# Preparing the weights of nine stages one stage earlier, in a chain of transformer layers on one core

## The reference

```python
h = tokens(x)                                    # sin/cos features times a matrix, class token in front
h = h + mixer_and_mlp(layernorm(h))              # layer 1
h = h + attention_and_experts(layernorm(h))      # layer 2
h = h + spiking_attention(layernorm(h))          # layer 3
h = h + attention_and_mlp(layernorm(h))          # layer 4

# layer 1:  x += mixer(rms(x) * g) @ w_out;  x += gelu(rms(x) * g @ ff_w1 + b1) @ ff_w2 + b2
# layer 2:  x += softmax(q k / 4) v @ out_proj.T + b, 12 heads of 16;  then 8 experts, the best 2 of each token
# layer 3:  branch(u, i) = spike(bn(u @ W[i].T + b[i]) / 2 - 1), bn of stored mean and variance
#           q, k, v = branches 0 to 2;  xa = (q k') v;  out = branch(spike(xa), 3)
# layer 4:  as layer 2's attention; the second half of the batch is a sum of three variants of fewer channels,
#           weighted by gumbel_weights[i]; then an MLP, for the second half again three weighted variants
```

## Time and profile before

| | us |
|---|---|
| median of 3 runs | 1893.24 |
| lowest and highest | 1886.21, 1893.82 |
| the profiled execution, its own time | 1889.81 |
| its span, first to last instruction | 1888.0 |
| TensorE busy | 1555.5 (82%) |
| VectorE busy | 1316.2 (70%) |
| ScalarE busy | 1046.0 (55%) |
| POOL busy | 412.8 (22%) |
| mean granted clock of TensorE | 0.858 |

### The profile page before, as it was taken

How to read it: one execution, slowest core, us unless ns; L and a number is a source line. 1 busy time by engine, 2 the same in 40 slices (tenths; PEclk the granted TensorE clock), 3 DMA queues, 4 the chain that set the end, 5 groups by cost and what they waited for, 6 DMA issues and landing times. The chain is left out here.

```text
span 1888.0 us, 37391 instructions
## 1 busy us (share of the span) xinstructions
PE 1555.5 (82%) x14612; PEld 1170.4 (62%) x14612; DVE 1316.2 (70%) x2862; ACT 1046.0 (55%) x1849; POOL 412.8 (22%) x419
## 2 busy tenths in 40 slices
PE   5898995867379889898999738993478989998896
PEld 5888985866246577673444627993476644445674
DVE  6888995499546545648996756883665469993566
ACT  7988994323546516355898225662100548984465
POOL 0000000000377510129950107672000310000100
PEclk9999997788555589997999858997788979997997
DMA  5121001000000000004520352221100000000101
GB/s 135 27 64 35 2 2 34 14 4 1 1 1 2 8 20 13 11 1 151 177 77 2 101 187 57 62 59 54 50 0 1 10 1 2 2 2 4 32 1 34
DMA packets 52571, 68.02 MB, mean 36 GB/s; under 512 B 11368, under 2 KB 41302, under 8 KB 52396
## 3 DMA queue, kind: packets, MB, share of 16 engines
q1 hardware_dynamic: 46418, 50.72, 8.8%
q0 software_dynamic: 3840, 9.18, 1.7%
q10 hardware_dynamic: 2138, 5.72, 1.2%
HBM read 46.97 MB, written 18.65 MB: 35 GB/s over the span
## 5 line engine op out<-in xcount | busy, mean ns | idle before, releaser
L1915 DVE TENSOR_REDUCE att_max<-banks 104x1 f32<-104x512 f32 (+1 forms) x480 | 295.9, 682 | 16.0 <-PE banks L1830 11.9
L1950 ACT ACTIVATE att_p<-banks 104x514 f32<-104x514 f32 (+1 forms) x480 | 261.9, 599 | 33.0 <-PE banks L1873 22.0
L339 PE MATMUL banks<-tok_wT,feature_halves 128*128 128x192 f16 x2592 | 228.8, 249 | 22.9 <-DVE feature_halves L365 11.8
L339 PEld LDWEIGHTS banks<-tok_wT,feature_halves 128*128 128x128 f16 x2592 | 216.6, 99 | 32.0 <-DVE feature_halves L365 17.6
L134 PE MATMUL banks<-ones 128*128 128x256 f16 x872 | 121.7, 311 | 92.7 <-PEq L113 50.4
L134 PEld LDWEIGHTS banks<-ones 128*128 128x128 f16 x872 | 96.2, 111 | 117.7 <-issue 92.4
L1889 PE MATMUL banks<-att_p,att_v 104*32 104x257 f32 (+1 forms) x1920 | 159.3, 404 | 0.9 <-ACT att_p L1950 0.3
L1873 PE MATMUL banks<-att_q,att_kT 64*104 64x257 f16 (+1 forms) x960 | 155.9, 303 | 2.9 <-ACT att_p L1950 2.5
L1830 PE MATMUL banks<-att_kT,att_q 64*104 64x512 f16 (+1 forms) x480 | 127.9, 429 | 10.1 <-POOL att_last_keys L1797 8.0
L1873 PEld LDWEIGHTS banks<-att_q,att_kT 64*104 64x104 f16 (+1 forms) x960 | 61.8, 123 | 106.3 <-ACT att_p L1950 79.7
L365 DVE TENSOR_TENSOR feature_halves<-features,feature_halves 128x2048 f16<-128x2048 f32 x54 | 123.4, 2284 | 5.8 <-ACT feature_halves L462 5.8
(11 more groups left out here) (462 smaller groups left out, 3541.6 us busy)
## 6 DMA issues: line engine op xcount, KB each, us to landing
expert_w_in<-in_L_ffn_w_dram SPq DMA_DIRECT2D x16, 576.0 KB, 4.6
expert_w_halves<-expert_w_halves SPq DMA_DIRECT2D x32, 288.0 KB, 2.6
tok_w<-in_L_tok_W_dram ACTq DMA_DIRECT2D x4, 1152.0 KB, 7.2
expert_w2s<-expert_w_halves SPq DMA_DIRECT2D x1, 4608.0 KB
expert_y<-expert_out SPq DMA_DIRECT2D x6, 513.0 KB
expert_w1s<-expert_w_halves SPq DMA_DIRECT2D x2, 1536.0 KB
raw<-in_x_dram SPq DMA_DIRECT2D x2, 1152.0 KB, 5.4
expert_w1s<-expert_w_halves SPq DMA_DIRECT2D x3, 768.0 KB
```

The costliest lines, as they stand in the source:

```text
L339: ins = pe.matmul(c.bank[t // 2][:, (t % 2) * D:(t % 2 + 1) * D], fh[:, s, q, z, t * 128:(t + 1) * 128], wT[:, y, k, 6 * q + wf, :], start ...
L1915: dve.reduce_max(mx[0:qn, n // NS % 2, 2 * gi + e, k:k + 1], bank_of(unit)[0:qn, 0:KEYS], X).then_inc(maxed, 1)
L1950: act.activation(p[0:kn, n % 4, :, :], c.pair[2 + n % 2][0:kn, :].rearrange("p (e q) -> p e q", e=2)[:, :, 0:HALF], ACT.Exp, scale=scale). ...
```

## The change

Each set of weights becomes an object (`Ahead`) with methods that are called inside the stage in front: `load` by SP, `turn` by TensorE, `place` or `scale` by ScalarE, `high` by ScalarE and `low` by VectorE inside the norm with `split`, `set` and `finish` by POOL, `fold` by VectorE. Weights of the mixer's projections, both MLPs and both attentions go into the norm in front; the output of the mixer is loaded during the chain; the spiking weights are loaded during the experts and folded during the combine; both output projections of heads are made with the attention weights or on POOL during attention. Attention's zeroed tiles are set by POOL during the QKV stage. The stages of preparation and the filler in front of these stages go.

```diff
 # norm
                 if ahead:
+                    ahead.load(sp)              # behind the gain loads
                     if split and par == 0 and ch:
                         low_part(eng, ch - 1, 0)
+                        if ch in (3, 4):
+                            ahead.low(eng, ch - 3)
...
                         eng.copy(split.h[:, 0:2, cols], split.x[:, :, cols]).then_inc(high, 1)
+                        if ch == 0:
+                            ahead.high(eng)
...
+                if ahead and not split:
+                    ahead.place(act)            # ScalarE, in front of its square roots
...
-                spin(c, pe, 120 if residual and kind else 60)
+                spin(c, pe, 60)
+                if ahead and not split:
+                    ahead.turn(pe)
+                if residual and kind:
+                    spin(c, pe, 50)
 # mixer_project: loads moved; "spin(c, pe, 36)" removed.  mixer_chain:
+        @block.sync
+        def _(sp):
+            sp.dma_start(wo[:, :, :], c.ins["L0_attn_w_out"]...).then_inc(wo_in, 16)
...
-            spin(c, pe, 36)
 # to_tokens, mixer's output
-                spin(c, pe, 20)
-                pe.wait_ge(w_in, 16 * len(loads))
+                pe.wait_ge(loaded, 16)
 # MlpWeights; mlps loses its loads, split_weights and "spin(c, pe, 90)"
+    def high(self, act):
+        act.wait_ge(self.w1_in, 48)
+        act.activation(self.w1[:, 0:2, :], self.w1f[:, :, :], ACT.Copy, scale=W_SCALE).then_inc(self.w_high, 1)
+        act.wait_ge(self.w2_in, 16)
+        act.activation(self.w2[:, :, 0, :], self.w2f[:, :, :], ACT.Copy, scale=W_SCALE).then_inc(self.w_high, 1)
+    def low(self, dve, part):    # part 0: two subtractions for w1, part 1: one for w2
...
 # Att0Weights
+    def turn(self, pe):          # 12 + 4 transposes of rows, then waits for the evictions
...
+        pe.wait_ge(self.placed, 7)
+    def place(self, act):        # 6 + 1 copies out of the banks
...
 # Att1Weights.finish: POOL, behind the last keys in attention
+        for k in range(2):
+            pool.tensor_scalar(w[0:DH + k, 1, k, :], w[0:DH + k, 0, k, :], g[0:DH + k, 0:1], 1.0, ...)
...
 # qkv: "spin(c, pe, 30)", the loads and the turning removed; POOL:
+                    if n == 2:
+                        pool.memset(att.mexp[:, :, :, :, :], 0.0).then_inc(att.set, 1)
+                    if n == 4:
+                        pool.memset(att.mx[:, :, :, :], 0.0).then_inc(att.set, 1)
+                        pool.memset(att.last[:, :, :, :], 0.0).then_inc(att.set, 1)
 # attention: POOL's fills and the waits of TensorE and VectorE for them removed
+                    if g == 0:
+                        pe.wait_ge(init, 2)     # only ahead of the first product with the last keys
 # moe_experts: SP runs SpikeWeights.load (11 loads).  moe_combine:
+                after.load_bias(sp)             # behind the six loads of expert rows
+            @block.scalar
+                after.scale(act)                # 2 square roots, 8 scalings, 8 copies
+            @block.tensor
+                after.turn(pe)                  # 16 transposes
             @block.vector
             def _(dve):
+                after.fold(dve)                 # in front of the additions
 # SpikeWeights: bias rows on four lanes of 192 in c.xT, moved by four loads into wT
+        self.pr = c.xT[64:68, 0, 0:5 * D].rearrange("p (k n) -> p k n", k=5)
 # spiking: the stage of preparation removed, with "spin(c, pe, 80)"
 # out_proj0 and small_proj removed; attention_layer calls heads_out itself
```

More of the change, by code:

```diff
@@ L504, in first_terms, with norm @@
     return [(0, 0, rows), (2, 0, rows), (0, 2, rows)]
-def norm(c, name, outer, kind, gains, biases=None, residual=False, split=None):
+def norm(c, name, outer, kind, gains, biases=None, residual=False, split=None, ahead=None):
     nc = c.nc
@@ L600, in _ @@
                         low_part(pool, ch, 1)
+                elif ahead:
+                    ahead.set(pool)
             @block.vector
@@ L699, in mixer @@
         dsk = c.sb(ctx, "D_skip", [128, 3])
-        mixer_project(c, sg, vT, coef)
+        with ExitStack() as inner:
+            win = MixerWeights(c, inner)
+            norm(c, "mixn", True, "rms", ["L0_attn_norm1_w"], ahead=win)
+            mixer_project(c, sg, vT, coef, win)
         gs = c.sb(ctx, "G_s", [128, 2 * LANES, L])
@@ L748, in _ @@
         def _(pe):
-            if loads:
-                spin(c, pe, 20)
-                pe.wait_ge(w_in, 16 * len(loads))
+            if loaded is not None:
+                pe.wait_ge(loaded, 16)
             for i in range(NTILE):
@@ L1583, in qkv, with __init__ @@
+class AttentionTiles:
+    def __init__(self, c, ctx, name):
+        self.mx = c.sb(ctx, name + "_max", [128, 2, 4, len(KT)])
+        self.mexp = c.sb(ctx, name + "_max_placed", [128, 2, 2, len(KT), 128], F16)
+        self.idh = c.sb(ctx, name + "_ident", [128, 128], F16)
+        self.last = c.sb(ctx, name + "_last_keys", [128, HEADS // 2, BATCH, 2], F16)
+        self.set = c.sem(name + "_set")
+def qkv(c, name, wts, q2, kT, v, att):
     nc = c.nc
@@ L1960, in _, with ff0, attention_layer @@
                 copy_sums(2 * G - 1)
-def ff0(c, x):
-    i = c.ins
-    mlps(c, "ff0", x, [dict(w1=i["L0_attn_ff_w1"], b1=i["L0_attn_ff_b1"], w2=i["L0_attn_ff_w2"], b2=i["L0_attn_ff_b2"],
-                            terms=ALL_TERMS, n=D, gain=None, chunks=range(NCH))],
-         ACT.Gelu_apprx_tanh)
-def attention_layer(c, name, w_qkv, b_qkv, project):
+def ff0(c, x, wts):
+    mlps(c, "ff0", x, wts, [dict(terms=ALL_TERMS, n=D, gain=None, chunks=range(NCH))], ACT.Gelu_apprx_tanh)
+def attention_layer(c, name, wts, weights):
     with ExitStack() as ctx:
@@ L2592, in _, with moe_experts @@
                 own.did(dve.tensor_scalar(comes[:, :], second, 0.0, None, ALU.max))
-def moe_experts(c, w1s, w2s, eid, goes, comes):
+def moe_experts(c, w1s, w2s, eid, goes, comes, after):
     nc = c.nc
@@ L2616, in moe_experts, with _ @@
         with nc.Block() as block:
+            @block.sync
+            def _(sp):
+                after.load(sp)
             @block.gpsimd
@@ L2804, in spiking @@
+def spiking(c, wts):
     nc = c.nc
```

580 lines of the change are left out of this document (278 added, 302 removed).

## The result

The changed kernel takes **1841.5 us** (median of four runs, 1840.4 to 1847.8); the kernel before, on the same chip, 1892.3. The ratio is 0.976, 95% interval 0.973 to 0.978: 51 us faster, 10.5 above the forecast of 1831 and inside its range. The profiled execution of the changed kernel is the slowest of its four, 1847.8 with a span of 1846.0; against the one before (1889.8, span 1888.0) it is 42.0 faster, where the terms summed to 58.8.

The account below looks back on a forecast made before the run. No single engine was taken to bound the kernel: every stage ends in a barrier, with TensorE, VectorE or a DMA bounding the work inside in turn. The terms summed to 58.8 us, 1889.8 - 58.8 = 1831, range 1818 to 1848.

Parts of the forecast that it names:

- Spiking: Spiking layer: preparation block goes, projections start 21.7 us earlier and warm (2.2), fold hidden in the combine; 23.9 us won.
- Output of heads: Output of heads after both attentions: one block and boundary fewer, starts 3.5 and 4.6 us earlier; 9.3 won for two.
- Attention starts: Start of both attentions: TensorE no longer idle 4.01 us until POOL sets its tiles; 3.0 each, 6.0 us for two.
- the attention norm: Norm before attention: ScalarE's copies delay its square-root table load, ready at 781.1 where the root ran at 780.48; -0.6 us.
- Only two projections slip in ahead: QKV stages: two projections run before POOL's fills end, first turn 1.3 us after them; 3.2 and 1.0 us won.
- Rival B: Moved work returns its saving: MLP norms grow by 10.4, a pause drops the clock in both QKV stages; 1845 us, 17%.
- 13 per us at 0.50: Mixer projections: 144 narrow matmuls, cold from the first, take 11.1 us and end at 347.1, not 351.9; 4.8 us won.
- Expert stage: Start of the expert stage: eleven loads share SP with the first gathers, for which TensorE waits; -0.7 us (-2 to 0).
- About 1.2 of the cold start goes as well: Output of heads, first attention: TensorE was at full rate before, so about 1.2 us of the cold start also goes.
- MLPs: First and last MLP: preparation moves into norms, which grow 5.6 and 6.6; products start earlier but cold; 5.9 and 4.5 won.
- A: Rival: the clock doesn't come back in the QKV stages, each 47 us longer at 1.2 GHz; 1925 us, slower, 3%.
- C: Rival: attention and heads start still warm after dense work, saving up to four restarts of 2.2 us; 1822 us, 15%.

Follow-up runs that it names:

- their own experiment: Weights of the two outputs of heads prepared in blocks of their own again behind each attention, against the changed kernel: 1854.9 us, 0.980.
- the experiment: Attention's zeroed tiles set at the head of attention again, all else as in the changed kernel: 1851.7 us, 0.979.
- The second trace: The changed kernel itself run and traced once more, nothing changed: 1844.6 us, 0.976 to the kernel before.

## Why the prediction was right, and where it was wrong

The time came from where it was looked for, and the largest terms held. *Spiking* was 23.1 for 23.9, in three parts (21.4 earlier, 2.5 warm, -0.8 in the output, which started at 0.50 as before but stayed there longer); the warm part is not in every execution. The fold lay inside the wait of the combine, as worked out from the earlier trace rows. *Output of heads*: the two starts gave 3.5 and 4.6, as forecast, and 3.6 and 4.6 by their own experiment. *Attention starts* gave 6.1 for 6.0 (3.2 and 2.9), 5.2 by the experiment, *mixer output and chain* 1.6 for 1.5, the attention norm -0.1 for -0.6. The MLP norms grew by 6.4 and 6.5 for 5.6 and 6.6.

In the profiled pair, terms that nobody forecast pull both ways and nearly cancel: the two tails (-3.2 and +3.0), the heads behind the second (+1.6), router and dispatch (+1.9), the experts' rhythm (-3.8). That they do is luck, and so is a part of how near 1831 came.

These steps failed:

**"Only two projections slip in ahead", "from POOL's end to the first turn I take 1.3 us" (QKV, +3.2 and +1.0; measured about -0.8 and -2.2).** TensorE's wait for POOL stands behind the *first* projection in the code; I let it stand behind the second. With the wait there, the first turns stood 7.7 behind the start, as forecast (7.8), and the stages gave 4.15 and 3.4 more, so +3.3 and +1.2. What I had not seen at all is the second price of a pause: behind it TensorE works at 0.50 for 7.0 and 5.4 us more. Rival B had this pause as a cause, with 2 each, but by a fall of the clock; the clock was down already and stayed down.

**"13 per us at 0.50" (mixer's projections, 4.8; measured 0.75).** I took the rate from one window of 1 us in the earlier trace rows. Over 3 us of the same trace it is:

```profile
349.00:352.00 3.00, 3.00 (x32) 0.50 0.00 0
```

10.7 per us, so 144 take 13.5 (14.0 in the trace after) and not 11.1: 2.9 of the missing 4.0. The wide ones behind lose 0.6 more at 0.50, and the rest goes in waits of TensorE for VectorE. Started warm, the same matmuls give 6.6 us.

**Expert stage, -0.7.** The loads cost 0.3 to 0.9, so the price was right. What the forecast left out is the later clock in the first tiles, 1.4 us more in both traces of the changed kernel. Of the -3.9 in the table the first tile is -1.9 and the rhythm of that one execution -3.8; 1.8 come back around them. The second trace, with 10 slow tiles in place of 27, has -2.4 there. The medians gain 50.8 where the profiled pair gains 42.0; the rhythm can be a part of that, but executions without a trace don't show it.

**"About 1.2 of the cold start goes as well" (heads of layer 2; measured -1.3).** The stretch before it ran at 0.50 to its end, and the heads started cold for 5.7 us, against 3.4 before.

**MLPs, 5.9 and 4.5 (4.4 and 3.8).** The cold start costs 1.4 in both where I took 0.7, and the first norm was 0.8 longer than I had it. My own numbers for the last MLP give 4.2 (1784.9 - 1780.0 - 0.7), not 4.5.

Of the rivals, A did not come: the QKV stages are at 1.00 from 13.4 and 11.8 us on. C did not come either: of its four restarts only the heads of layer 4 were warm (1.6); the heads of layer 2 were cold, and both attentions began at 1.00 but fell to 0.50 within 4 us, for some 20 us. The kernel with filler in the norms starts QKV at 1.00, waits 4.2 us and goes on at 0.50. The Trainium skill (TensorE: Matmul & The Clock Gate, "Why this matters for your kernels") warns against idle gaps between bursts of matmuls for that reason, and this trace agrees. The changed kernel's gap of 2.24 us is no such case, since the clock was at 0.50 before it.

In the attention norm ScalarE's copies were done 8.7 us behind the start, not 9.5. Its table load began 0.02 behind them, and the square root ran 0.14 behind the load, 10.15 us from the start, as before. The Trainium skill (ScalarE: Activation LUTs, "What ACT_TABLE_LOAD costs") adds a drain of about 1.4 us to a switch; these rows show none.

## What to carry to other kernels

Preparing a stage's operands one stage early pays what the idle stretch was, if the new place has idle time on the same engine: beside the mixer's output the MLP split cost 0.1 us, in the norm 6.4. When a stage's head is emptied, look at what TensorE waits for next and let it do everything that does not need it first; a short wait behind a cold start costs itself and, as the QKV stages showed, a later rise of the clock. And put filler into the waits of the stage in front, not in front of the work: there it cost under 0.4 us in any norm here, and the mixer's projections and QKV started warm; behind the MLP norms a pause was left, and it gave 0.3 us and nothing.

## What the runs showed of the hardware

- Behind a cold start of a QKV stage the clock was at 1.00 after 6.6 and 5.0 us of work without a pause, and after 13.4 and 11.8 us where a pause of 2.24 us followed the first 4.2 us of work.
- The same 144 narrow matmuls, with 12 columns each, take 14.0 us from a cold start and 10.2 to 11.6 from a warm one, during which the clock falls from 1.00 to 0.50 although TensorE is busy all the time by the profile.
- The last 14 us of an attention ran at 0.50 or at 1.00 with the same work; the difference is 3.0 to 3.2 us there and 1.6 to 2.2 in the heads behind. Four traces of code that is the same up to there showed the same level, and moving a wait by one projection changed it.
- VectorE's copy of 128x1344 takes 0.86 or 1.03 us in the expert stage, and a tile takes 3.70 us or, for 4 to 27 of the 40 tiles, 3.8 to 4.1. POOL issues its indirect DMAs beside it; whether the two meet was not tried.
- The 72 transposes of the first MLP's norm took 12.0 us in most traces and 19 in three, at 0.50. The norm is then 6.8 to 8.1 us longer where the split is not in it (30.3 and 31.7 for 23.6), and 0.35 where it is (30.3 for 29.95). What tips it was not found.
- Beside a POOL subtraction of 1.16 us, two of VectorE's subtractions took 1.59 and 1.99 us (in the MLP norm); without one they took 0.96 and 1.36 (at the head of the MLP stage). Nothing else was tried there.
